# Moving 71 payload gathers of the target order out of the first attention hop, to the end of the scores and beside the four softmax scans

## The reference, cut to what matters

```python
scores = leaky_relu(s_h + s_t + s_r)            # per edge and head
att = segment_softmax(scores, head_ids, N)      # over the edges with one head node
A = 0.9 * att
for _ in range(5):                              # five hops
    msgs = A[:, :, None] * Z[tail_ids]
    Z = segment_sum(msgs, head_ids) + 0.1 * Z0
```

## Time and profile before

| | us |
|---|---|
| median of 3 runs | 12004.88 |
| lowest and highest | 11990.27, 12047.62 |
| the profiled execution: its own time | 12010.07 |
| its span | 12007.8 |
| POOL busy | 7991.8 (67%) |
| DVE busy | 6262.3 (52%) |
| PE busy | 5179.3 (43%) |
| ACT busy | 2459.6 (20%) |

### The profile page before, as it was taken

The page is one execution under the profiler, slowest core; times in us unless marked ns, Lnnn a source line. Parts: engine busy times, 40 slices in busy tenths (PEclk is TensorE's granted clock), DMA queues, the critical chain, the costliest instruction groups (busy, mean ns, idle before and its releaser), DMA issues. The chain is left out here.

```text
span 12007.8 us, 102357 instructions
## 1 busy us (share of the span) xinstructions
PE 5179.3 (43%) x22423; PEld 3584.6 (30%) x22423; DVE 6262.3 (52%) x12751; ACT 2459.6 (20%) x4317; POOL 7991.8 (67%) x7869
## 2 busy tenths in 40 slices
PE   1719994000000244445656678843335422222245
PEld 1403331000000144444444556622224322222234
DVE  8931115767878644465545669943336533321127
ACT  0102221022222211122323333310003200000035
POOL 1767774776767677753767666657767677777730
PEclk9959997555555555566767777755556555555578
DMA  2412222544545311167655556622229833311148
GB/s 107 165 20 58 57 58 72 167 136 151 165 149 166 104 40 42 41 215 211 168 155 167 178 185 191 194 75 59 59 54 312 246 65 65 65 47 46 46 152 251
DMA packets 1247797, 1471.21 MB, mean 123 GB/s; under 512 B 843713, under 2 KB 948738, under 8 KB 1244410
## 3 DMA queue, kind: packets, MB, share of 16 engines
q1 hardware_dynamic: 951992, 1127.40, 29.7%
q0 software_dynamic: 277328, 269.94, 10.7%
q10 hardware_dynamic: 18290, 72.03, 1.5%
HBM read 830.95 MB, written 772.36 MB: 134 GB/s over the span
## 5 line engine op out<-in xcount | busy, mean ns | idle before, releaser
L2541 POOL DMA_INDIRECT r_got<-state,comb_src x1176 | 1218.2, 1036 | 449.3 <-issue 350.1
L328 POOL DMA_INDIRECT payload_or_bias_rows<-payload,place x784 | 875.5, 1117 | 669.6 <-issue 260.4
L1330 POOL DMA_INDIRECT hop_got<-edges_b,next_col x784 | 790.7, 1009 | 271.8 <-issue 238.0
L1330 POOL DMA_INDIRECT hop_got<-edges_a,next_col x784 | 783.4, 999 | 265.5 <-issue 238.2
L1579 PE MATMUL hop_ps_into<-hop_out,span_s 128*128 128x256 f32 (+1 forms) x10 | 5.6, 660 | 2046.4 <-DVE hop_out L1471 2045.1
L1519 ACT COPY hop_got<-hop_zeros 128x1792 f32<-128x1792 f32 x224 | 377.4, 1685 | 1514.9 <-DVE hop_ps_msg L1422 1102.8
L1579 PEld LDWEIGHTS hop_ps_into<-hop_out,span_s 128*128 128x128 f32 x10 | 2.5, 311 | 2048.9 <-DVE hop_out L1471 2047.3
L1471 DVE SCALAR_TENSOR_TENSOR hop_out<-hop_out,hop_runs_now,hop_ps_msg 128x256 f32<-128x256 f32 x1176 | 565.5, 481 | 51.0
L1342 POOL DMA_INDIRECT sum<-hop_out,put_s x392 | 432.2, 1103 | 119.5 <-issue 119.5
L2678 DVE TENSOR_REDUCE r_stat<-r_sq 128x14 f32<-128x896 f32 x196 | 211.9, 1081 | 571.1 <-ACT r_sq L2848 570.8
L2549 POOL DMA_INDIRECT x<-r_yt,put_t x392 | 403.9, 1030 | 143.8 <-issue 118.9
(11 more groups left out here) (727 smaller groups left out, 16871.7 us busy)
## 6 DMA issues: line engine op xcount, KB each, us to landing
edges_a<-hop_out SPq DMA_DIRECT2D x112, 896.0 KB
edges_b<-hop_out SPq DMA_DIRECT2D x112, 896.0 KB
hop_side<-x_dst SPq DMA_DIRECT2D x280, 224.0 KB, 4.0
r_in<-state SPq DMA_DIRECT2D x112, 448.0 KB, 4.7
x_and_sums<-c_y SPq DMA_DIRECT2D x56, 896.0 KB, 5.6
bn_in<-x_and_sums SPq DMA_DIRECT2D x56, 896.0 KB, 4.9
r_own<-state SPq DMA_DIRECT2D x84, 448.0 KB, 5.3
g_rows<-r_gx SPq DMA_DIRECT2D x84, 448.0 KB, 2.9
```

The lines of the kernel that those rows point to most:

```text
L328: nc.gpsimd.indirect_dma_start(out=rows[:, n, :], out_offset=None, in_=t.pay, in_offset=bass.IndirectOffsetOnAxis(t.place[:, k, n:n + 1], ...
L1330: pool.indirect_dma_start(out=got[:, u, c, :], out_offset=None, in_=table, in_offset=at, bounds_check=EP - 1, oob_is_err=False).then_inc(g ...
L2541: pool.indirect_dma_start(out=got[:, n, c - b * CT, :], out_offset=None, in_=table, in_offset=bass.IndirectOffsetOnAxis(idx[:, at + c:at + ...
```

## The change

The first 71 of the 250 gathers leave hop 0. 27 are appended to POOL's program in `edge_scores`, behind its last gather. Each of the four softmax scans gets a POOL program with 11 of them. Hop 0 keeps the other 179. The two scans of the degrees, which come earlier, are called without `under` and stay as they were. Number, order and data of the gathers are the same.

```diff
+UNDER_SCORES = 27
+UNDER_SCAN = 11
 UNDER_HOP = 250
...
-def segment_scan(nc, t, name, factor, adds, outs, reverse, biggest=False):
+def segment_scan(nc, t, name, factor, adds, outs, reverse, biggest=False, under=None):
...
         block = ctx.enter_context(nc.Block())
+
+        if under is not None:
+            @block.gpsimd
+            def _(pool):
+                first = UNDER_SCORES + under * UNDER_SCAN
+                payload_rows(nc, t, t.raw, 1, range(first, first + UNDER_SCAN), t.got_t)
...
                         pool.indirect_dma_start(out=got[:, u, c, cols], out_offset=None, in_=rows,
                                                 in_offset=bass.IndirectOffsetOnAxis(by[:, at], 0)).then_inc(gathered[u], 16)
+            payload_rows(nc, t, t.raw, 1, range(UNDER_SCORES), t.got_t)
...
-        segment_scan(nc, t, "max_up", penalty[:], each(s), each(up), reverse=False, biggest=True)
+        segment_scan(nc, t, "max_up", penalty[:], each(s), each(up), reverse=False, biggest=True, under=0)
...
             if table is None:
-                payload_rows(nc, t, t.raw, 1, range(UNDER_HOP), t.got_t)
+                payload_rows(nc, t, t.raw, 1, range(UNDER_SCORES + 4 * UNDER_SCAN, UNDER_HOP), t.got_t)
```

More of the change, by code:

```diff
@@ L1196, in _ @@
                 nc.vector.tensor_tensor(pick[:], up[:], last, ALU.mult)
-        segment_scan(nc, t, "max_down", goes_on[:], each(pick), each(tot), reverse=True)
+        segment_scan(nc, t, "max_down", goes_on[:], each(pick), each(tot), reverse=True, under=1)
         with ExitStack() as c2:
@@ L1209, in _ @@
                 nc.scalar.activation(e[:], s[:], ACT.Exp)
-        segment_scan(nc, t, "sum_up", t.same_s[:], each(e), each(up), reverse=False)
+        segment_scan(nc, t, "sum_up", t.same_s[:], each(e), each(up), reverse=False, under=2)
         with nc.Block() as block:
@@ L1214, in _ @@
                 nc.vector.tensor_tensor(pick[:], up[:], last, ALU.mult)
-        segment_scan(nc, t, "sum_down", goes_on[:], each(pick), each(tot), reverse=True)
+        segment_scan(nc, t, "sum_down", goes_on[:], each(pick), each(tot), reverse=True, under=3)
         with ExitStack() as c2:
```

## The result

| | before | with the change |
|---|---|---|
| median | 12012.41 us (8 runs, 11990.27 to 12048.01) | 11975.59 us (8 runs, 11927.3 to 11992.61) |
| profiled execution, its span | 12007.8 | 11926.9 |
| POOL busy | 7991.8 (67%) | 7982.4 (67%) |
| DVE busy | 6262.3 (52%) | 6264.4 (53%) |

The ratio is 0.9962, 95% interval 0.9946 to 0.9979: 37 us, where 76 were forecast, and the median lies outside the range of 11907 to 11963. The pair of profiled executions alone shows 81. So two questions stand: which term was wrong in the trace, and why the runs show less than their trace.

A forecast was written before the change was run, and what follows sets the result against it. The prediction took POOL's gathers, running alone for 87.4 us at hop 0's end, as the bound. Terms -84.5 + 0 + 8.4 = -76.1 us from 12004.88 gave 11929 us, range 11907 to 11963.

The forecast's parts named there:

- the exit of a scan block: End of each scan block: the next operation starts 0.53 us behind the block's last work, read from DVE's row.
- the restart: From hop 0's fix to hop 1's first gather: kept at 12.26 us, as before the change.
- Hop 0, -84.5: End of hop 0: with 71 gathers fewer, the last store releases the fix 2.88 us behind `hop_add`; gain 84.5 us.
- The rival that something else holds the fix: Hop 0's end: late stores above all hold the fix until about 2432; time 12013, chance 0.03.
- Scores, 0: Behind the scores: 27 gathers end by about 1931.9, before POOL must arrive at 1936.5; cost nothing, bounds 0 to 2.4 us.
- Scans, 8.4: Four softmax scan blocks: 11 gathers beside each make POOL end 2.1 us too late per block; cost 8.4 us.
- The forecast called itself wrong if a scan block grew by over 3 us: Sign for the scan blocks: each should grow by 1.4 to 2.1 us; over 3 us would refute the prediction.
- the rival's 18.53: From hop 0's fix to hop 1's first gather: 18.53 us as behind hop 1; gain 69.8, time 11935, chance 0.27.
- neither reason given for the two: Behind hop 0's fix: long-idle engines have their next instructions at hand, or the POOL program that ran sets the time.
- The mean pace: Moved gathers take 1.77 us each, hop 0's mean, in scans and scores; gain 46.6, time 11958, chance 0.14.
- The chance of faster by over 0.5%, 0.73: Whole kernel: chance that the measurement shows a gain over 0.5%, 60 us, summed as 0.49 + 0.22 + 0.02.
- The rule of the Trainium skill: Scan blocks: gathers are not held up by DVE's tensor_tensor, so the scans cost 5.5 us and the time is 3 us lower.

The follow-up runs named there:

- h2: The kernel before, unchanged, run on chip E for its trace there; 12020.14 us.
- h3: The changed kernel with 20 of the scores' 27 gathers issued earlier, 8 beside each scan, 183 in hop 0, 150 in the dense stage; 11936.51 us, 0.9933.
- i1: The kernel before with UNDER_HOP = 183 in place of 250, nothing else, on chip F; 11930.96 us, ratio 0.9925.
- h1: The changed kernel run again on chip E as the base; 11954.53 us, ratio 0.9955 to the kernel before.
- f1: The kernel before, unchanged, run on chip C for its trace there; 14583.22 us in its 10 runs.

## Why the prediction was wrong, point by point

The step that failed in the mechanism is the exit of a scan block: it was priced at 0.53 us, as behind DVE, and measured 2.19 behind POOL's last gather, which makes the scans 14.7 us for 8.4. With the restart (15.74 for 12.26) and a later last gather of scores this takes 12 us from the gain. It is not what put the median outside the range: of the 47 us between forecast and median, 7.5 are a base that moved and some 27 a step between runs whose cause stays open.

- **Hop 0, -84.5: right.** The fix is 2.89 us behind `hop_add` for 2.88, and DVE's part kept its length. The rival that something else holds the fix is out.
- **Scores, 0: right on the chips of 12000, not in general.** There the stretch is 39.7, 48.6 and 39.8 us with the gathers, and the 9 us of the middle one go with TensorE's clock, which fell before them. On the chips of 14550 the term is 30 and more. The cover was right by its length: POOL was ready in time. The forecast asked only whether POOL ends in time, not what its gathers do to engines in the same block.
- **Scans, 8.4: the step that failed in the trace.** POOL's lateness was 2.0 us for 2.1, with one gather of 1.61 us. But the exit was taken from DVE's row, 0.53 us, and costs 2.19 us behind a gather (2.0 to 2.3 in the 32 such blocks of the eight traces with 11 gathers). Measured 14.7. The forecast called itself wrong if a scan block grew by over 3 us: `max_up` grew by 3.76.
- **Restart, 12.26 kept: 15.74.** Half way to the rival's 18.53, and explained by neither reason given for the two.
- **The sum, -76.1: -64.0.** That is the mean of three traces against two on chips of 12000. It is borne out by the times: over chips A, E and F the change has 23 executions with a mean of 11954.5 us, the kernel before 51 with 12018.5, a difference of 64.0 us (twice the standard error is 11), and the medians are 66.6 apart. The mean pace, the rival whose 46.6 us and 11958 lie nearest to the measured median, was not what happened: the gathers ran at 1.25 us.
- **The forecast of the median, 11929 with 11963 as upper end: 11975.59.** 7.5 us are the base: with eight runs the kernel before has 12012.41 where the forecast had 12004.88 from three. 12 more are missing in the sum. That leaves some 27. The eight runs on A are, in their order, three of 11927 to 11935 and then five of 11966 to 11993; the kernel before shows no such step (mean 12014 in its first three, 12021 in the other five). So the first three show a gain of 84 us and the other five 37. On E the change's runs reach from 11935 to 11984, on F from 11932 to 11952. A part of such scatter can be seen in the traces, ahead of the change: the scores' block starts on POOL at 861.4 to 862.8 us in five traces on these chips and at 881.8 to 883.0 in three (h2, h3 and i1; none of the change itself), one wait of DVE in the block ahead being 91.6 us in h2 for 69.2 in the first trace of before. Another part may be the clock in the stretch behind the scores, 4 to 9 us. Whether these two made the five runs of A is open, since only the first of A's executions of the change has a trace. The range allowed 20 us below and took its upper end from a rival's mechanism; scatter of the same 20 to 40 us above was not in it.
- **The chance of faster by over 0.5%, 0.73.** Measured were 0.38% on A, 0.45% on E, 0.65% on F, and 0.15 to 0.30% on the slower chips. With the gain of 64 us that the traces show, on a bound of 60, this was a coin's toss, not three in four.
- **The rule of the Trainium skill** ("SBUF — State Buffer", section "Who interferes with whom"), that a tensor_tensor takes only the read side of the shared ports and so, as the page infers, leaves descriptor generation alone: by it the scans would have cost 5.5 us in the forecast's sum. Beside the scans one gather in eleven took 1.61 us and the others 0.94, so the forecast's allowance of 0.7 us a block was right. The one of 1.61 started at 1960.57 inside the last scan (1960.39 to 1961.43) and ended 0.75 behind it. Beside hop 0's tensor_tensor the 2.67 us of the earlier trace rows stand again, which speaks against the rule as it is put, and the measurement decides. The exit mattered more than either.

## What to carry to other kernels

When work is put on another engine beside a bound one, take the block's exit from a row where that engine ends last with that kind of instruction; an exit behind an indirect DMA's issue cost 2.2 us where one behind VectorE cost 0.5, and with 11 gathers that alone was 1.7 of the 3.7 us a block. Before work is spread over several gaps, look for one stage with enough idle time on the engine: here one number, 183 for 250, brought what four scan programs and a tail brought, on the chips where the dense stage has that cover. And an engine that "ends in time" can still slow its neighbours while it works, by nothing in the traces of three chips and by 30 us in those of three others, so such a term needs a bound above nothing. When one trace shows a stretch longer by a few us, look at the granted clock in it before the change is blamed: in h1 the clock had fallen before the first moved gather.

## What the runs showed of the hardware

- The same kernel takes 12010 to 12024 us on three chips and 14554 to 14581 on three others. The scores' block shows it best: it starts on POOL at 861 to 863 or 882 to 883 us on the former and 1203 to 1205 on the latter, and from there to the reload it takes 1075 and 1423 us (first trace of before, f1; 1409 to 1490 over the twelve traces of B, C and D). The mean granted clock is 0.638 to 0.641 in the traces of the former and 0.612 to 0.616 in those of the latter.
- On the chips of 14550 a 128-row gather of 32-byte rows beside the dense stage costs 1.24 us (321 against 142 of them; 1.35 with 213 on another of these chips), close to the 1.25 from one gather's start to the next; on those of 12000, 67 more cost nothing.
- Beside the scans of 128x392 ten of `max_up`'s eleven gathers took 0.94 us and one, in the last set, 1.61. In hop 0 the gather that starts inside DVE's 2.02 us multiply of two SBUF tiles ends 0.81 to 0.83 us behind it in each of the 56 steps, before and after; the longest take 2.67.
- Among the four scan blocks, those whose last work is POOL's indirect DMA are left 2.0 to 2.3 us behind that gather's end, those whose last work is DVE's 0.52 to 0.55 us behind it.
- From the fix to the next hop's first gather: 10.3 us with no gathers ahead of it in the block (one trace), 15.5 to 16.1 with 179 that end 4.6 us ahead of `hop_add`'s end or 183 that end 0.5 behind it (sixteen traces), 12.2 to 12.3 with 250 that run up to the fix (three).
